# A transformer block on one core: GpSimd prepares the next tile's rows ahead of the power of the output rows' statistics

## What is computed

```python
h = _layernorm(x) * (1 + ca) + sa
# the mixer
x_shift = roll(h, -512, rows) @ Wts.T * g + h * (1 - g)
xn = layernorm(x_shift) * ln_w + ln_b
k, v = xn @ Wk.T, xn @ Wv.T
states = scan(s * exp(time_decay) + exp(-exp(time_first) * sigmoid(k)) * v)
x = x + ga * (states @ Wo.T)
# the feed-forward part
h = _layernorm(x) * (1 + cb) + sb
shared = silu(h @ Wsg) * (h @ Wsu) @ Wsd * sigmoid(h @ Wse)
x = x + gb * (shared + experts of the 4 best of 32, by h @ Wr)
```

## Time and profile before

| what | value |
|---|---|
| median of 3 runs | 720.41 us |
| the profiled execution: its own time | 720.49 us |
| its span, from the first instruction to the last | 718.7 us |
| TensorE busy | 672.3 us, 94% of the span |
| DVE, ACT, GpSimd busy | 367.4, 288.9, 185.1 us |
| mean granted clock of TensorE | 0.976 of full speed |

### The profile page before, as it was taken

The page is one execution under the profiler, slowest core; times in us unless marked ns, Lnnn a source line. Parts: engine busy times, 40 slices in busy tenths (PEclk is TensorE's granted clock), DMA queues, the critical chain, the costliest instruction groups (busy, mean ns, idle before and its releaser), DMA issues.

```text
span 718.7 us, 8895 instructions
## 1 busy us (share of the span) xinstructions
PE 672.3 (94%) x3218; PEld 466.0 (65%) x3218; DVE 367.4 (51%) x714; ACT 288.9 (40%) x552; POOL 185.1 (26%) x174
## 2 busy tenths in 40 slices
PE   4798688999998899998999899999999999999997
PEld 3665455767676667886665566666666666667875
DVE  3779677678678877763214223122122243225755
ACT  3445775665656633323225124233232343323231
POOL 1254565645536200001122022222221212120000
PEclk9899978999999999999999999999999999999999
DMA  7670200001232008206777767878899787816311
GB/s 276 232 250 0 76 15 30 15 31 30 74 122 84 15 1 281 85 1 242 266 231 239 257 217 253 263 238 280 271 322 339 239 270 261 284 22 234 117 49 69
DMA packets 50295, 118.27 MB, mean 165 GB/s; under 512 B 6904, under 2 KB 11084, under 8 KB 50252
## 3 DMA queue, kind: packets, MB, share of 16 engines
q1 hardware_dynamic: 45388, 109.31, 43.0%
q0 software_dynamic: 4864, 8.40, 5.4%
HBM read 100.87 MB, written 18.91 MB: 167 GB/s over the span
## 4 chain that ended last, share of the span: by engine, by line
PE 61%; DVE 5%; DMA 3%; ACT 2%; issue 2%; POOL 2%; SPq 0%; DVEq 0%; ACTq 0%; POOLq 0%
PE bank L1686 28%; PE bank L1698 11%; PE bank L1741 11%; PE bank L1758 6%; DMA egu<-in_L_ffn_Wu_dram 2%; PE bank L1729 1%; ACT xsH L860 1%; DMA xg<-h_rows,slot_tok 1%; PE bank L1789 1%; PE bank L1747 1%; DVE xres L1260 1%; DVE prodL L1224 1%; POOL ho L634 1%; DVE prod L1222 1%; POOL xres L642 1%
## 5 line engine op out<-in xcount | busy, mean ns | idle before, releaser
L1686 PE MATMUL bank<-xsH,wguH 128*128 128x512 f32 x352 | 143.8, 408 | 1.7 <-DVE xsL L1214 1.3
L1686 PE MATMUL bank<-xsL,wguH 128*128 128x512 f32 x352 | 138.0, 392 | 0.0
L1686 PE MATMUL bank<-xsH,wguL 128*128 128x512 f32 x352 | 137.7, 391 | 0.0
L1741 PE MATMUL bank<-egu,xeT 128*64 128x352 f32 x512 | 80.9, 469 | 3.3 <-DMA egu<-in_L_ffn_Wu_dram 3.3
L1686 PEld LDWEIGHTS bank<-xsH,wguH 128*128 128x128 f32 x352 | 66.6, 189 | 26.4 <-issue 10.8
L1222 DVE TENSOR_TENSOR prod<-bank,silu 128x512 f32<-128x512 f32 x38 | 26.2, 690 | 110.7 <-PE bank L1686 87.7
L1698 PE MATMUL bank<-wdH,prodH 128*128 128x512 f32 x176 | 73.7, 419 | 6.3 <-DVE prodL L1224 4.1
L692 POOL DMA_INDIRECT expert_sums<-ye,slot_to x32 | 49.2, 1537 | 116.7 <-DMA expert_sums<-ye,slot_to 92.0
L1686 PEld LDWEIGHTS bank<-xsL,wguH 128*128 128x128 f32 x352 | 66.3, 188 | 14.7
L1686 PEld LDWEIGHTS bank<-xsH,wguL 128*128 128x128 f32 x352 | 66.6, 189 | 13.0 <-issue 0.7
L699 POOL DMA_INDIRECT xg<-h_rows,slot_tok x16 | 16.8, 1050 | 221.3 <-ACT ye L899 90.2
(11 more groups left out here) (222 smaller groups left out, 1020.8 us busy)
## 6 DMA issues: line engine op xcount, KB each, us to landing
egu<-in_L_ffn_Wg_dram SPq DMA_DIRECT2D x32, 704.0 KB, 6.2
egu<-in_L_ffn_Wu_dram SPq DMA_DIRECT2D x32, 704.0 KB, 7.7
ed<-in_L_ffn_Wd_dram SPq DMA_DIRECT2D x32, 512.0 KB, 5.2
h2T<-in_L_wmod_dram SPq DMA_DIRECT2D x6, 1024.0 KB, 8.7
ed<-in_L_ffn_Wd_dram SPq DMA_DIRECT2D x32, 192.0 KB, 6.3
h_rows<-ho SPq DMA_DIRECT2D x16, 256.0 KB, 2.0
expert_sums<-ye SPq DMA_DIRECT2D x16, 256.0 KB, 8.9
out_dram<-xres SPq DMA_DIRECT2D x16, 256.0 KB, 2.2
```

What stands on the lines that cost most here:

```text
L1686: ins = mm.matmul(bk[:, :], l[f][:, w, c, :], r[:, c, :], start=(k == 0), stop=(k == 3 * C - 1))
L1741: ins = mm.matmul(bk[side, 0:F], xeT[:, c, side], egu[:, e, w, c, :], start=(c == 0), stop=(c == C - 1))
```

## The change

In each step `out_rstd(t - 5)` goes behind `mix_rows(t + 1)`. Both are done in steps 5 to 14, so ten powers move behind ten pairs of additions and products; in steps 15 to 20 there is no next tile, and the order is the same. No instruction, semaphore, transfer or buffer is added or taken away.

```diff
                 for t in range(STEPS):
                     if t < NT:
                         mixed_rstd(t)
-                    if 0 <= t - 5 < NT:
-                        out_rstd(t - 5)
                     if t == 0:
                         first_rstd(5)
                     if t + 1 < NT:
                         mix_rows(t + 1)
+                    if 0 <= t - 5 < NT:
+                        out_rstd(t - 5)
                     if t >= 7:
                         scale_sum(t - 7)
                         h2_rows(t - 7)
```

## The result

In the first comparison the changed kernel took 726.51 and 724.09 us against a median of 719.85: a ratio of 1.008 (95% interval 1.0049 to 1.0111), some 5.8 us. (A ratio here is not the quotient of the two medians, which lie 10.95 us apart in this case.) The first comparison had left out two runs of it, at 735 us, as disturbed; since the second has such a time too (734.89, at the same mean clock of 0.965), its six runs are the better base, and with all four the first median is 730.95. The forecast was 727.1 us, 6.6 us slower, in a range of 721 to 731: the sign is right, and the size lies between the two comparisons. By the better base the median of 731.13 stands just past the upper end of the range.

What follows compares the result with a forecast made beforehand. The mixer's loop through `veh`, `rsh`, `nbh`, `ho` and `hT` was taken to set the pace, the dense end hardly absorbing lateness. Additions of 13.8 us less returns of 7.2 gave 6.6 us later, 727.1 us, range 721 to 731.

Steps and rivals of the forecast that it cites:

- dense part as much later as the end: Sign to look for: the dense part runs as much later as the kernel's end, 6.6 us in the forecast.
- The price of one move: Step 11: `rsh` 1.0 us later behind the pair, plus 0.4 for `scale_rows` beside it: 1.4 a step, ends 1.0 and 1.7.
- step 10: Mixer step 10: ACT later by 1.4 + 0.4 = 1.8 us, as the pair's wait for `xhat` now precedes the power.
- step 9: Mixer step 9: 0.4 us of lateness, 1.04 being hidden by a wait for statistics; return of 2.4 from a shorter `xsL`.
- step 7: Mixer step 7: 2.3 us later, 1.4 for the move and 0.9 as the power meets DVE's split of weights.
- Step 16's return of 0.3: Step 16: TensorE's wait for `prodL` shrinks a little as GpSimd overlaps it less, 0.3 us back.
- Step 13: xsL 4.21 against 2.50: 1.7: Step 13: DVE's `xsL`, no longer stretched by GpSimd, gives back 1.7 us; the step's own lateness was 0.7.
- more gaps, lower clock: Rival: longer and new TensorE gaps, in steps 12, 13 and 16, lower its clock; 2.5 to 4 us more, 730 us; chance 0.12.
- The bare price: Rival: each move costs only its bare 1.0 us; additions 8.8 less 7.2, +1.6 us, 722.1 us; chance 0.15.
- The faster case: Rival: TensorE, dense from step 10 on, covers ACT's lateness while the returns of 7.2 us stay: 716.3 us; chance 0.07.
- sign of being wrong: ACT's wait for `rsh` stays near 9 us, or grows while TensorE's idle time up to 190 us does not.

Runs made afterwards that it cites:

- e4: Changed kernel with the power one instruction further back, behind the scaling of `xres`, in steps 7 to 14: 736.56 us, 1.0231 of before.
- e1: Kernel of before with the power behind the pair in steps 5 to 9 only: 723.36 us against 718.89, ratio 1.0065.
- e2: Kernel of before with the power behind the pair in steps 10 to 14 only: 725.33 us, ratio 1.0088.
- e9: The changed kernel unaltered, timed again beside other kernels (the second comparison): median 731.13 us against 720.18, ratio 1.0141.
- e11: Changed kernel with spare matmuls ahead of two expert-stage waits, for the first pair's rows and the fourth pair's weights: 731.37 us, 1.0166 of before.
- e10: Kernel of before with order chosen by step: old in 5, 6, 10, 12; power between the pair in 7, 8, 11, 13, 14; changed in 9: 715.39 us, 0.9951.
- e12: The kernel with the order chosen by step, plus spare matmuls ahead of two expert-stage waits: 715.33 us, 0.9949 of before.
- e3: Kernel of before with the power between the pair's two instructions in steps 5 to 14: 719.86 us, ratio 0.9982.
- e6: Kernel of before with the power behind the pair in steps 9 and 13 only: 718.31 us, ratio 0.9989.
- e7: Changed kernel with seven spare matmuls on TensorE ahead of its wait for the scan in step 12: 725.56 us, 1.0083 of before.
- e8: Changed kernel with the old order in step 12 alone: 726.18 us, 1.0098 of before.

## Why the prediction was right, point by point

**What bounds the kernel.** That the loop `veh`, `rsh`, `nbh`, `ho`, `hT` sets the pace of the mixer and the dense part hands its lateness on held: e4 lengthened only that loop and lost 16.6 us. The table's sums against the times are 4.0 and 4.7 (e1), 5.5 and 6.3 (e2), 15.5 and 16.6 (e4), 10.0 and 10.1 (e9), 11.3 and 11.9 (e11), -4.0 and -3.5 (e10), -4.1 and -3.7 (e12). For the two smaller gains it is not shown: -2.9 and -1.3 (e3, an interval of -3.5 to 0.8), -2.6 and -0.8 (e6, -2.4 to 0.8). A single profile misleads here: the one of the changed kernel was 9 us behind before from 185 us to some 335 us and 6 us behind from 421 on, because three things were longer in the profile of before: the wait for the first fetched rows near 338 us (2.44 us against 1.61), the wait for weights near 395 us (3.30 against 2.86), and the 32 matmuls behind it, with the clock lower (6.61 against 4.95). The forecast's "dense part as much later as the end" therefore does not hold in this profile.

**The price of one move.** 1.4 us, of which 0.4 was a guess from 0.62 for `scale_rows` beside the pair. Step 11 shows 4.16 - 2.73 = 1.43, and the pair's second instruction stretched by 0.48. That instruction was issued at 144.15 and `scale_rows` held DVE from 144.08 to 144.76; had it waited out all of that, as the rule cited in the prediction says (the Trainium skill, SBUF — State Buffer, "Who interferes with whom"), it would have ended at 144.76 + 1.29 = 146.05. It ended at 145.92. So the trace agrees with that rule but for 0.13 us, and the taken 0.4 was a little low.

**The steps.** In step 10 the 1.8 came out as 1.94 where the steps ahead had the old order (e2) and as 2.6 behind the changed step 9: there the pair waited 1.25 us for `xhat` (the 1.3 in the waits above), in e2 0.51, in the forecast 0.34. In step 7 the lateness of `rsh` was as forecast (5.09 us behind the start of `rsx` against 2.74), but a return was overlooked: the next `negx`, which GpSimd had stretched to 0.69, took 0.16 again, and DVE's 0.17 of waiting for `mx` fell away, 0.7 us of the 0.75 missing. Step 16's return of 0.3 is not seen: TensorE's wait of 0.81 for `prodL` is gone, but the changed kernel is 9.02 us behind at step 15's `rsx` and 9.01 behind at the same matmul near 230 us.

**The term that failed** is "Step 13: xsL 4.21 against 2.50: 1.7", as a return: the `xsL` did become 1.71 shorter, but the step became 1.50 us longer where the sum had it 1.0 shorter. The instruction came sooner to its end only in its own length; ahead of it DVE now waited 4.00 us for `xsH`, because TensorE ran at the lower level and ACT, which makes `xsH`, waited 2.49 us for the router's logits. The sum had the clock at nothing. This is the third rival, "more gaps, lower clock", which had named step 12 as a place of a new gap and priced it at 2.5 to 4 us; there it cost 2.5 us in e9 and the first profile and 4.4 in e11. Not every fall costs: near 104 to 107 us the clock falls in the changed kernel, e7, e8 and e11 and not in e1 and e9, and step 8 is as long in all six (+0.76 to +0.78). The rival had 0.12 of the chance, and deserved more: the sum of the steps without it is 6.9, e7 with the clock held in step 13 measures 6.8, and the changed kernel as it is 9.3 to 10.0. That 6.9 and 6.8 agree so well is luck in part, since steps 7 and 10 miss by 0.8 each in opposite directions; and that the first comparison's two runs came near 727.1 is luck too, since the six later runs put the kernel some 10 us above before.

**The rivals.** The bare price (+1.6 us) is out: it had additions of 8.8, and ACT's wait alone grew by 14.7. The faster case is out: e2 shows that TensorE does not cover the second half. But its mechanism exists, since GpSimd's getting out of DVE's way is worth 1.2 to 2.0 us in step 9 alone, and e10 turns it into a faster kernel. In the forecast's own terms, the move is good where something else holds the power's reader up anyway, and bad elsewhere.

**What it would show.** No idle time ahead of `rsh` in steps 5 to 8 and 10 to 14 (right), 3.7 to 4.2 us behind `rsx` (3.66 in step 5 and 4.11 to 4.16 in steps 11 to 14; but 4.63, 5.09 and 4.55 in steps 6 to 8 and 5.37 in step 10), ACT's wait of 15 us or more (23.5), longer waits of DVE for `hT` (19.5 instead of 12.3), `xsL` of 2.9 and 2.5 (2.95, 2.50). TensorE's idle time grew from 11.1 to 14.7 us between 55 and 120 us and from 2.8 to 3.7 between 120 and 190, so neither sign of being wrong came. Step 11's `rsx` should start 4 to 6 us later: 142.27 against 136.84, 5.4.

## What to carry to other kernels

Ask of each instruction that is moved back who waits for it at once, and of each that is moved forward what it will stand beside; price both per step, since one and the same exchange was worth from -1.9 to +2.6 us from step to step here, and the choice step by step beat both uniform orders. A lateness that opens a gap on TensorE ahead of work that sets the pace can cost twice: the gap, and then the lower clock behind it, which cost 2.5 us here and made a loss of 1.5 of a gain of 1.0. Compare the lengths of steps between profiles, not one profile's span: a whole profile carried some 3 us of chance from waits for rows and weights and the clock behind them.

## What the runs showed of the hardware that was not expected

- An idle time of TensorE of 1.77 us, 11 us behind the end of another of 1.56, was followed by a clock of 0.53 from 165 to 170 us and 0.79 in the 5 us after; with 1.75 us of spare matmuls in its place, or with 0.49 us of it left, the clock stayed at 1.00. But a wait of 3.69 us for weights in e8, near 400 us, was followed by no fall (the 32 matmuls took 4.95), and one of 2.65 in e4 was (6.64). Length of the wait alone does not decide it.
- Spare matmuls of 1.75 us ahead of a wait made the product behind that wait 0.09 us later at most (e7).
- The same fall of the clock has a price or none by what waits for TensorE: 2.5 us in step 13 and nothing in step 8 of the changed kernel; in e4 a wait of 4.10 us for `prodL` was followed by a clock of 0.50 from 155 to 160 us, and steps 11 and 12 were longer only by what `rsh` was later.
- A DVE instruction of one column with two SBUF operands, `negh`, took 0.29 to 0.61 us instead of 0.16 while GpSimd's 512-column instructions ran beside it (changed kernel; up to 1.18 in e4), and `negx` 0.16 where it had been stretched to 0.69 and 0.82.
- The four transfers of the fourth pair's weights took from 11.1 us (e10) to 15.2 (e6) from the first one's issue to the matmuls that wait for them. Why is open.
